# A graph kernel's row gathers issued without a write behind each, without waits for those writes, and at most two pairs ahead of TensorE

## The chip, the cores and the metric

The kernel runs on one core of a Trainium2 chip. The metric is the device time of one execution in microseconds. Of the kernel before there are three timed runs, and one further execution that the hardware profiler recorded.

## What is computed

A node has 128 features, there are 12500 nodes and 212500 edges `src -> dst`, sorted by `dst`, each of one of eight relation types. The kernel computes two relational layers, a layer norm, a graph layer with degree scaling and a second layer norm. Cut to what matters:

```python
def _rgcn_layer(x, W, SW, b, src, dst, rel):
    xt = jnp.einsum('nd,rde->rne', x, W)
    agg = jax.ops.segment_sum(xt[rel, src], dst, num_segments=x.shape[0])
    return jax.nn.relu(agg + x @ SW + b)
# L0: x1 = rgcn(x, w1, ...); x2 = rgcn(x1, w2, ...)       (sums 1 and 2)
x = _layernorm(x + L0(x))
# L1: feat = relu(x @ W1 + b1); h = feat * deg ** -0.5
#     agg = segment_sum(h[src], dst)                      (sum 3)
#     y = (feat - agg * deg ** -0.5) @ W2 + b2
x = _layernorm(x + L1(x))
```

So there are three sums over all edges, one after the other, and each needs, for every edge, the row of 128 floats of its source node: rows of `x` in sum 1, of `x1_d` in sum 2, of `h_d` in sum 3.

## The kernel before

**Gathers.** The edges are cut into 1661 tiles of 128. One gather, an indirect DMA issued by GpSimd (POOL), brings the 128 source rows of one tile from DRAM into one slot of `rows`, which has 56 slots. Seven tiles (`KG`) are a group, two groups (`PAIR`) a pair of 14 tiles, four pairs (`PR`) one pass of 56 tiles, which is once round the ring of slots. A sum has 29 full passes (`IT`) and a last one (`LEFT`) of 14, 14 and 9 tiles. 14 gathers of sum 2 and 21 of sum 3 are issued at the end of the sum before by `early` (L772); the other 4948 come from `run` (L802).

**What orders POOL's work.** `Gathers.run` is POOL's whole program in a sum, in order. Ahead of a pair it waits for `idx_ready` (ScalarE has copied the 14 columns of indices) and for `summed` (TensorE has used up the pair that decides). Which pair that is, `lead` says: with `lead=PR` it is the same pair of the pass before, so that POOL can be four pairs ahead of TensorE; with `lead=NEAR`, which is 2, it is the pair two before. The kernel before has `lead=PR` in passes 0 to 26, `NEAR + 1` in pass 27 and `NEAR` in pass 28 and in `LEFT`. Behind every gather stands a write of zeros to `pause`, which nobody reads (L806). The last write of a group (sums 1 and 2) or of a pair (sum 3) increments `paused`, and POOL waits for it ahead of the next one (`self.rest`).

**TensorE.** It waits for a whole group of landed rows, multiplies each tile with its one-hot matrix `r_S` (L990 in sums 1 and 2, L1214 in sum 3; an fp32 product is two MATMUL records, so a pair is x28), and signals `summed`. In sums 1 and 2 it runs in every pass, between pairs 0 and 1, the eight products with the relation weights (`mix`, L965), and around the pairs the steps of a tail that finishes 436 nodes. VectorE builds `r_S` for a pair when the pair two before is summed (L1051, L1244), adds the results into `acc`, and does the tail's elementwise work.

**Joins between sums.** `early` waits for the tail's stores (`stored`) and for `summed`; the next sum's other work waits for `over`, that is for all stores of the sum.

Of the kernel before, what the change touches and what calls it, by code (L numbers as in the profile page):

```python
# [12 lines left out]
P = 128  # L13
# [6 lines left out]
KG = 7  # L20
# [3 lines left out]
RING = 8  # L24
# [95 lines left out]
def build(nc, x, src, dst, rel, w1, sl1, b1, w2, sl2, b2, gw1, gb1, gw2, gb2, out):  # L120
    with ExitStack() as top:
        def sb(name, shape, dt=F32):
            return top.enter_context(nc.sbuf_tensor(name, shape, dt))


        def scratch(name, *shape):
            return nc.dram_tensor(name, shape, F32, kind="Internal").ap()

        x1_d, part_d, h_d = (scratch(n, N, D) for n in ("x1_d", "part_d", "h_d"))
        dinv_d = scratch("dinv_d", NPAD)  # L130


        c = Shared()
        c.W = [sb("w1s", [P, NREL, D]), sb("w2s", [P, NREL, D])]
        c.SL = [sb("sl1s", [P, D]), sb("sl2s", [P, D])]
        c.B = [sb("b1s", [P, 1]), sb("b2s", [P, 1])]
        c.GW = [sb("gw1s", [P, D]), sb("gw2s", [P, D])]
        c.GB = [sb("gb1s", [P, 1]), sb("gb2s", [P, D])]
        c.ident = sb("ident", [P, P])
        c.zeros_bf = sb("zeros_bf", [P, P], BF16)  # L140
        c.one_bf = sb("one_bf", [P, 1], BF16)
        c.eps = sb("eps", [P, 1])
        c.src_i = sb("src_i", [P, NT + UN], I32)
        c.rows = sb("rows", [P, UN, D])
        c.idx = sb("idx", [P, SETS * UN], I32)
        c.node = sb("node", [P, NT])
        c.relf = sb("relf", [P, NT])
        c.lo_b = sb("lo_b", [P, NT])
        c.glo = sb("glo", [P, NG])
        c.key = sb("key", [P, NT])  # L150
        c.gs = sb("gs", [P, NG])
        c.off_i = sb("off_i", [1, NGP, OFFS], I32)
        c.gs_i = sb("gs_i", [1, RING + NG], I32)
        c.gs8 = sb("gs8", [1, NG])
        c.step_t, c.step_g, c.carry = sb("step_t", [P, 1]), sb("step_g", [P, 1]), sb("carry", [P, 1])
        c.pause = sb("pause", [P, PT, P])
        c.found = sb("found", [SPOTS, DEG_COLS + COLS])
        c.deg = sb("deg", [DEG_ROWS, DEG_PARTS, NODES])
        c.dinv = sb("dinv", [P, NB])
        c.acc = sb("acc", [P, ACC])  # L160
        c.rounds_i = sb("rounds_i", [1, 2], I32)
        c.top = top
        c.passed = top.enter_context(nc.semaphore("passed"))
        c.over = top.enter_context(nc.semaphore("over"))
        c.psum = [top.enter_context(nc.psum_tensor(f"bank{i}", [P, BANK], F32)) for i in range(8)]
        c.iota = c.psum[IOTA_BANK][:, 0:TK]

        loads = [(c.W[0], w1.rearrange("r i o -> i r o")), (c.W[1], w2.rearrange("r i o -> i r o")),
                 (c.SL[0], sl1), (c.SL[1], sl2), (c.GW[0], gw1), (c.GW[1], gw2),
                 (c.B[0], b1.rearrange("(p a) -> p a", a=1)), (c.B[1], b2.rearrange("(p a) -> p a", a=1)),  # L170
                 (c.GB[0], gb1.rearrange("(p a) -> p a", a=1)), (c.GB[1], gb2.partition_broadcast(P))]
        c.early = early = Early(nc, top, c)
        last = Gathers(nc, top, c, "r3", h_d, 1, 2, 1, None)
        second = Gathers(nc, top, c, "r2", x1_d, 0, 1, PAIR, last)
        first = Gathers(nc, top, c, "r1", x, 0, 0, PAIR, second)
        with ExitStack() as ctx:
            prologue = Prologue(nc, ctx, c, early, Blocks(nc, ctx), (dst, src, rel), loads)
            tail = Tail1(nc, ctx, c, x, x1_d)
            one = relational_sum(nc, ctx, c, "r1", first, c.W[0], tail, prologue, None)
        with ExitStack() as ctx:  # L180
            tail = Tail2(nc, ctx, c, x, x1_d, part_d, h_d, dinv_d)
            two = relational_sum(nc, ctx, c, "r2", second, c.W[1], tail, None, early)
        with ExitStack() as ctx:
            tail = Tail3(nc, ctx, c, part_d, out)
            three = plain_sum(nc, ctx, c, last, tail, early)
        block = top.enter_context(nc.Block())

        @block.sync
        def _(sync):
            one.sync(sync)  # L190
            two.sync(sync)
            three.sync(sync)

        @block.scalar
        def _(act):
            one.scalar(act)
            two.scalar(act)
            three.scalar(act)

        @block.gpsimd  # L200
        def _(pool):
            one.gpsimd(pool)
            two.gpsimd(pool)
            three.gpsimd(pool)

        @block.tensor
        def _(pe):
            one.tensor(pe)
            two.tensor(pe)
            three.tensor(pe)  # L210

        @block.vector
        def _(dve):
            one.vector(dve)
            two.vector(dve)
            three.vector(dve)
# [484 lines left out]
class Gathers:  # L701
# [3 lines left out]
    def __init__(self, nc, top, c, tag, table, which, turns, incs, then):  # L705
        def sem(name):
            return top.enter_context(nc.semaphore(f"{tag}_{name}"))

        self.c, self.table, self.which, self.incs = c, table, which, incs
        self.most = N // GN + 2 if which else 4 * (N // GN + 1) + 1  # L710
        self.turns, self.then = turns, then
        self.rest = PAIR if then is None else 1
        self.landed = [sem(f"landed{h}") for h in range(RING + PAIR)]
        assert [s.num - self.landed[0].num for s in self.landed] == list(range(RING + PAIR))
        self.cleared = sem("cleared")
        self.paused = sem("paused")
        self.idx_ready = sem("idx_ready")
        self.summed = sem("summed")

# [56 lines left out]

    def run(self, pool, ready, stored):

        rest = self.rest

        def iteration(q, i, part, set_of, skip=0, lead=PR):
            at = set_of * UN
            for p in part.pairs:
                if (p + 1) * PT <= skip:
                    pool.sem_inc(self.paused, PAIR // rest)
                    continue
                pool.wait_ge(self.idx_ready, (q * (IT + 1) + i) * PR + p + 1)
                pool.wait_ge(self.summed, self.pairs_summed(q, i, p + PR - lead))  # L788
                gate(pool, self.c.passed)
                for h in range(p * PAIR, (p + 1) * PAIR):  # L790
                    if (h + 1) * KG <= skip:
                        if h % rest == rest - 1:
                            pool.sem_inc(self.paused, 1)
                        continue
                    if h % rest == 0:
                        pool.wait_ge(self.paused, q * (NG // rest) + i * (RING // rest) + h // rest + 1)  # L796
                        gate(pool, self.c.passed)
                    for k in range(part.of(h)):
                        s, slot = h * KG + k, h if k < halves(part, h) else RING + h % PAIR
                        if s < skip:  # L800
                            continue
                        pool.indirect_dma_start(  # L802
                            out=self.c.rows[:, self.place(s), :], out_offset=None, in_=self.table[:, :],
                            in_offset=bass.IndirectOffsetOnAxis(ap=self.c.idx[:, at + s:at + s + 1], axis=0)
                        ).then_inc(self.landed[slot], 16)
                        ins = pool.memset(self.c.pause[:, s % PT, :], 0.0)  # L806
                    if h % rest == rest - 1:
                        ins.then_inc(self.paused, 1)

        def one_round(q, skip=0):  # L810
            iteration(q, 0, FULL, 0, skip)
            with pool.Fori(0, IT // SETS - 1) as n:  # L812
                i = pool.snap(n * SETS)
                iteration(q, i + 1, FULL, 1)
                iteration(q, i + 2, FULL, 0)
            iteration(q, IT - 2, FULL, 1, lead=NEAR + 1)
            iteration(q, IT - 1, FULL, 0, lead=NEAR)
            iteration(q, IT, LEFT, 1, lead=NEAR)

        self.begin(pool)  # L820
        pool.sem_inc(self.cleared, 1)
        pool.sem_inc(self.paused, 1)
        one_round(0, EARLY[self.turns])
        if ready is not None:
            pool.wait_ge(ready, 1)
# [10 lines left out]
                pool.sem_inc(self.cleared, 1)  # L836
                one_round(q)
        pool.end_ifs()
        pool.wait_ge(self.paused, rounds * (NG // rest) + 1)
        gate(pool, self.c.passed)  # L840
        if self.then is not None:
            self.early(pool, rounds, stored)

# [976 lines left out]
```

## Time and profile before

| | |
|---|---|
| median of 3 runs | 7126.02 us (7123.88 to 7126.11) |
| profiled execution, its own time | 7141.85 us |
| its span | 7140.1 us |
| POOL busy | 5849.0 us (82%) |
| TensorE busy (matmul records) | 3398.9 us (48%) |
| VectorE / ScalarE busy | 1707.3 / 692.0 us |
| DMA share, mean of 16 engines, in each sum | 0.20, 0.20, 0.19 |

Engines are PE (TensorE), PEld (its weight loads), DVE (VectorE), ACT (ScalarE), POOL (GpSimd) and SP (SyncE). A row of a timeline gives the start, the duration, the engine, the line, the operation, and in brackets how long the engine had been idle before it and what ended that. A letter q behind an engine's name is its instruction queue. A POOL record of a gather covers the work of making it, not the landing of its data.

### The profile page before, as it was taken

To read this page: it belongs to the slowest core of one execution; us is meant where nothing else is said; L and a number is where in the kernel's file an instruction comes from. 1 tells how busy PE (TensorE), PEld (TensorE's weight loads), DVE (VectorE), ACT (ScalarE), POOL (GpSimd) and SP (SyncE) were. 2 spreads that over 40 slices of the span, in tenths; PEclk is the share of its full clock that TensorE was granted. 3 is DMA by queue.
4 is the path that set the end of the run, shared out by engine and by line. 5 is a ranking of instruction groups with operands and counts; after the bars stand their busy time and mean duration, and the time that the engine had idled before them with its cause. 6 is when DMAs were issued, how large, how long until landed. Compare 5 with 4: busy or idle time off the path is not lost.

```text
span 7140.1 us, 55913 instructions
## 1 busy us (share of the span) xinstructions
PE 3398.9 (48%) x12908; PEld 2515.0 (35%) x12909; DVE 1707.3 (24%) x2844; ACT 692.0 (10%) x1395; POOL 5849.0 (82%) x9940
## 2 busy tenths in 40 slices
PE   4455445554445655555554555554333333333333
PEld 3333333333333433333333333344333333333333
DVE  5333333333333312222222222221111111111111
ACT  2111111111111211111111111110000000000000
POOL 8888888888888788888888888878888888888887
PEclk7667666776667767777777777775555555555555
DMA  2111111111111212212222122221111111111111
GB/s 67 52 51 51 50 51 52 50 50 51 51 52 52 53 51 57 57 55 56 58 56 56 55 57 57 56 59 51 53 53 52 52 54 52 52 53 54 52 52 53
DMA packets 197671, 382.92 MB, mean 54 GB/s; under 512 B 84402, under 2 KB 93406, under 8 KB 197622
## 3 DMA queue, kind: packets, MB, share of 16 engines
q0 software_dynamic: 159456, 326.88, 17.5%
q1 hardware_dynamic: 36496, 54.67, 2.2%
q10 hardware_dynamic: 1670, 0.85, 0.0%
q8 instruction: 14, 0.23, 0.0%
q14 instruction: 35, 0.29, 0.0%
HBM read 356.43 MB, written 25.65 MB: 54 GB/s over the span
## 4 chain that ended last, share of the span: by engine, by line
POOL 78%; issue 20%; PE 1%; POOLq 1%; DMA 0%; DVE 0%; ACT 0%; DVEq 0%; SPq 0%; ACTq 0%
POOL rows L802 63%; POOL pause L806 15%; PE bank L965 0%; PE bank L990 0%; POOLq L112 0%; POOL rows L772 0%; PE bank L299 0%; DMA rows<-x_d,idx 0%; POOLq L788 0%; PE bank L1214 0%; PE bank L286 0%; POOLq L796 0%; DMA rows<-in_x_dram,idx 0%; POOLq L812 0%; DMA rows<-h_d,idx 0%
## 5 line engine op out<-in xcount | busy, mean ns | idle before, releaser
L990 PE MATMUL bank<-r_S,rows 128*128 128x128 f32 x6644 | 1361.7, 388 | 2125.9 <-DMA rows<-in_x_dram,idx 1065.1
L990 PEld LDWEIGHTS bank<-r_S,rows 128*128 128x128 f32 x6644 | 1259.3, 292 | 2271.9 <-issue 2271.6
L802 POOL DMA_INDIRECT rows<-in_x_dram,idx x1661 | 1587.6, 956 | 449.9 <-issue 258.2
L802 POOL DMA_INDIRECT rows<-x_d,idx x1647 | 1573.4, 955 | 444.0 <-issue 253.9
L802 POOL DMA_INDIRECT rows<-h_d,idx x1640 | 1565.0, 954 | 366.9 <-issue 272.0
L1214 PE MATMUL bank<-r_S,rows 128*128 128x64 f32 x3322 | 767.8, 424 | 1468.3 <-DMA rows<-h_d,idx 1462.0
L1214 PEld LDWEIGHTS bank<-r_S,rows 128*128 128x128 f32 x3322 | 726.2, 330 | 1513.7 <-DMA rows<-h_d,idx 925.2
L806 POOL MEMSET pause<- 128x128 f32 x4948 | 1097.1, 222 | 4.0
L1051 DVE TENSOR_TENSOR r_S<-bank,key 128x1792 f32<-128x1792 f32 x238 | 480.4, 2019 | 1219.8 <-PE bank L990 1219.2
L917 ACT COPY r_agg<-bank 128x512 f32<-128x512 f32 x476 | 278.2, 584 | 3961.9 <-PE bank L965 2066.5
L1271 DVE TENSOR_TENSOR acc<-acc,bank 128x64 f32 x238 | 52.9, 222 | 1920.2 <-PE bank L1214 1904.4
L965 PE MATMUL bank<-r_agg,w1s 128*128 128x512 f32 (+1 forms) x528 | 458.5, 1037 | 4.5 <-ACT bank L580 4.5
L965 PE MATMUL bank<-r_agg,w2s 128*128 128x512 f32 (+1 forms) x528 | 457.8, 1035 | 4.7 <-ACT bank L580 4.7
L1046 DVE TENSOR_TENSOR r_hot<-bank,b_spot 128x1344 bf16<-128x1344 f32 x119 | 185.4, 1558 | 1145.0 <-PE bank L990 1142.7
L1090 DVE TENSOR_TENSOR acc<-acc,bank 128x64 f32 x492 | 109.2, 222 | 802.3 <-PE bank L965 745.6
L1049 DVE TENSOR_REDUCE r_placed<-r_hot 128x192 bf16<-128x1344 bf16 x119 | 288.3, 2422 | 4.1
L580 ACT CAST bank<-zeros_bf 128x512 f32<-128x512 bf16 x480 | 282.1, 588 | 21.4 <-DVEq L571 6.4
L965 PEld LDWEIGHTS bank<-r_agg,w1s 128*128 128x128 f32 x528 | 115.2, 224 | 319.5 <-issue 319.3
L965 PEld LDWEIGHTS bank<-r_agg,w2s 128*128 128x128 f32 x528 | 113.1, 218 | 317.8 <-issue 317.3
L746 ACT COPY idx<-src_i x360 | 71.2, 202 | 1015.7 <-PE bank L1214 964.6
L1244 DVE TENSOR_TENSOR r_S<-bank,key 128x896 f32<-128x896 f32 x119 | 129.8, 1092 | 36.4 <-DVE acc L1271 36.3
L1746 ACT ACTIVATE d_sd<-d_mv,eps 109x4 f32<-109x4 f32 (+2 forms) x29 | 8.6, 297 | 1277.0 <-DVEq L1766 1277.0
(151 smaller groups left out, 1384.4 us busy)
## 6 DMA issues: line engine op xcount, KB each, us to landing
rows<-in_x_dram,idx POOLq DMA_INDIRECT x1661, 2.6
rows<-x_d,idx POOLq DMA_INDIRECT x1647, 3.5
rows<-h_d,idx POOLq DMA_INDIRECT x1640, 2.5
d_xr<-in_x_dram SPq DMA_DIRECT2D x54, 218.0 KB
x_d<-d_yr SPq DMA_DIRECT2D x27, 218.0 KB
d_x1r<-x_d SPq DMA_DIRECT2D x27, 218.0 KB
h_d<-d_hr SPq DMA_DIRECT2D x27, 218.0 KB
part_d<-d_pr SPq DMA_DIRECT2D x27, 218.0 KB
```

The lines of the kernel that those rows point to most:

```text
L580: return act.copy(ap, c.zeros_bf[0:ap.shape[0], 0:1].broadcast_to([*ap.shape]))
L802: pool.indirect_dma_start(out=self.c.rows[:, self.place(s), :], out_offset=None, in_=self.table[:, :], in_offset=bass.IndirectOffsetOnAxis ...
L806: ins = pool.memset(self.c.pause[:, s % PT, :], 0.0)
L917: act.copy(agg[:, h, :, :], agg_ps[h % BUFS][:, :].rearrange("p (n r) -> p n r", r=NREL)).then_inc(taken, 1)
L965: mm = pe.matmul(mix_ps[:, 0:groups * GN], W[:, r, :], agg[:, first:first + groups, :, r], start=(r == 0), stop=(r == NREL - 1))
L990: mm = pe.matmul(agg_ps[j][:, bass.ds(offs[j * KG + k], TK)], c.rows[:, g.place(h * KG + k), :], S[:, pb, j * KG + k, :], start=False, sto ...
L1046: ch.then(dve.tensor_tensor(hot[:, b, :, :], spots.unsqueeze(1).broadcast_to([P, PT, SPOTS]), bc_last(blocks.spot[:, at], SPOTS), ALU.is_e ...
L1049: dve.tensor_reduce(placed[:, b, :, :], hot[:, b, :, :].rearrange("p (j k) n -> p j n k", k=KG), AX.X, ALU.add)
L1051: dve.tensor_tensor(S[:, b, :, :], c.iota[:, :].unsqueeze(1).broadcast_to([P, PT, TK]), bc_last(c.key[:, at], TK), ALU.is_equal).then_inc( ...
L1090: ins = dve.tensor_tensor(window, window, mix_ps[:, w * GN:(w + 1) * GN], ALU.add)
L1214: mm = pe.matmul(sum_ps[b][:, j * GN:(j + 1) * GN], c.rows[:, g.place(h * KG + k), :], S[:, b, j * KG + k, :], start=(k == 0), stop=(k == ...
L1244: dve.tensor_tensor(S[:, p % BUFS, :, :], c.iota[:, 0:GN].unsqueeze(1).broadcast_to([P, PT, GN]), bc_last(c.key[:, bass.ds(i * UN + p * PT ...
```

## The change

The writes to `pause`, the buffer, the semaphore `paused`, its increments and all waits for it go away. The passes 1 to 28, an even number, are all in one loop and all have `lead=NEAR`; pass 0 keeps `lead=PR` and `LEFT` keeps `NEAR`. The gathers themselves, their tables, indices, slots and semaphores stay.

```diff
-        c.pause = sb("pause", [P, PT, P])
...
-        self.rest = PAIR if then is None else 1
...
                 pool.wait_ge(self.idx_ready, (q * (IT + 1) + i) * PR + p + 1)
                 pool.wait_ge(self.summed, self.pairs_summed(q, i, p + PR - lead))
                 gate(pool, self.c.passed)
                 for h in range(p * PAIR, (p + 1) * PAIR):
-                    if (h + 1) * KG <= skip:
-                        if h % rest == rest - 1:
-                            pool.sem_inc(self.paused, 1)
-                        continue
-                    if h % rest == 0:
-                        pool.wait_ge(self.paused, q * (NG // rest) + i * (RING // rest) + h // rest + 1)
-                        gate(pool, self.c.passed)
                     for k in range(part.of(h)):
...
                         ).then_inc(self.landed[slot], 16)
-                        ins = pool.memset(self.c.pause[:, s % PT, :], 0.0)
-                    if h % rest == rest - 1:
-                        ins.then_inc(self.paused, 1)
...
             iteration(q, 0, FULL, 0, skip)
-            with pool.Fori(0, IT // SETS - 1) as n:
+            with pool.Fori(0, IT // SETS) as n:
                 i = pool.snap(n * SETS)
-                iteration(q, i + 1, FULL, 1)
-                iteration(q, i + 2, FULL, 0)
-            iteration(q, IT - 2, FULL, 1, lead=NEAR + 1)
-            iteration(q, IT - 1, FULL, 0, lead=NEAR)
+                iteration(q, i + 1, FULL, 1, lead=NEAR)
+                iteration(q, i + 2, FULL, 0, lead=NEAR)
             iteration(q, IT, LEFT, 1, lead=NEAR)
...
-        pool.wait_ge(self.paused, rounds * (NG // rest) + 1)
-        gate(pool, self.c.passed)
```

On POOL, where pass 0 of sum 1 ends and the loop over the passes begins, the rows before are these (`rows` is the ring of slots, `r1_` marks a semaphore of sum 1):

```order
L802 DMA rows<-in_x_dram,idx 128x128
L806 MEMSET pause 128x128
L812 UNCONDITIONAL_BRANCH
L812 ISA
L788 ISA [waits r1_idx_ready]
L796 REGISTER_ALU [waits r1_summed]
L802 DMA rows<-in_x_dram,idx 128x128 [waits r1_paused]
L806 MEMSET pause 128x128
```

In the changed kernel, where L789 is the gather and the loop is L796, the same place reads:

```order
L789 DMA rows<-in_x_dram,idx 128x128 x13
L796 UNCONDITIONAL_BRANCH
L796 ISA
L782 ISA [waits r1_idx_ready]
L789 DMA rows<-in_x_dram,idx 128x128 [waits r1_summed]
L789 DMA rows<-in_x_dram,idx 128x128 x13
```

Gathers now follow each other directly, and a pair's first gather has the waits for `idx_ready` and `summed` alone; the value that `summed` must reach there is two pairs higher. The order of the instructions on TensorE, VectorE, ScalarE and SyncE is the same in both kernels but for the line numbers.

## Rows read from the trace of the kernel before

**Rows 1.** The page: busy time by engine, and the chain that ended last

```profile
PE 3398.9 (48%) x12908; PEld 2515.0 (35%) x12909; DVE 1707.3 (24%) x2844; ACT 692.0 (10%) x1395; POOL 5849.0 (82%) x9940
...
POOL 78%; issue 20%; PE 1%; POOLq 1%; DMA 0%; DVE 0%; ACT 0%; DVEq 0%; SPq 0%; ACTq 0%
```

**Rows 2.** Groups of POOL instructions: line, operation, count | busy us, mean ns

```profile
L802 POOL DMA_INDIRECT rows<-in_x_dram,idx x1661 | 1587.6, 956 | 449.9 <-issue 258.2 <-POOL pause L806 191.6
...
L806 POOL MEMSET pause<- 128x128 f32 x4948 | 1097.1, 222 | 4.0
```

**Rows 3.** Waits of POOL, whole span: us in total, times, longest us

```profile
POOL rows L802 <- issue: 784.2, 4358, 2.6
POOL rows L802 <- POOL pause L806: 476.5, 589, 0.9
```

**Rows 4.** Timeline of POOL in the middle of sum 1

```profile
1028.54 0.95 POOL L802 DMA_INDIRECT rows<-in_x_dram,idx  x1 [0.81 <-POOL pause L806]
...
1029.87 0.95 POOL L802 DMA_INDIRECT rows<-in_x_dram,idx  x1 [0.16 <-issue]
...
1036.57 0.95 POOL L802 DMA_INDIRECT rows<-in_x_dram,idx  x1 [0.17 <-issue]
```

**Rows 5.** The gathers of L772, and their timeline ahead of sum 2

```profile
L772 POOL DMA_INDIRECT rows<-h_d,e_idx x21: 943/947/952, 4808.3 to 4833.3; - x21
...
2407.80 0.95 POOL L772 DMA_INDIRECT rows<-x_d,e_idx  x1 [2.43 <-issue]
...
2424.07 0.95 POOL L772 DMA_INDIRECT rows<-x_d,e_idx  x1 [0.30 <-issue]
2425.32 0.94 POOL L802 DMA_INDIRECT rows<-x_d,idx  x1 [0.30 <-issue]
```

**Rows 6.** Timeline of POOL: first and last gather after a gap of 1.07

```profile
171.56 0.96 POOL L802 DMA_INDIRECT rows<-in_x_dram,idx  x1 [1.07 <-issue]
...
7118.72 0.95 POOL L802 DMA_INDIRECT rows<-h_d,idx  x1 [1.07 <-issue]
```

**Rows 7.** Timeline of POOL: first gathers of pass 0 and pass 1, sum 1

```profile
4.53 1.10 POOL L802 DMA_INDIRECT rows<-in_x_dram,idx  x1 [2.63 <-issue]
...
89.21 0.95 POOL L802 DMA_INDIRECT rows<-in_x_dram,idx  x1 [0.82 <-POOL pause L806]
```

**Rows 8.** Timeline of PE in pass 0 of sum 1

```profile
69.89 4.97 PE L990 MATMUL bank<-r_S,rows 128*128 128x128 f32 x28
74.70 14.86 PE L965 MATMUL bank<-r_agg,w1s 128*128 128x512 f32 x16
...
97.34 3.37 PE L990 MATMUL bank<-r_S,rows 128*128 128x128 f32 x28
```

**Rows 9.** Timeline of PE at the start of sum 2, pairs 0 to 2

```profile
2444.80 5.33 PE L990 MATMUL bank<-r_S,rows 128*128 128x128 f32 x28 [9.52 <-issue]
...
2466.47 8.16 PE L990 MATMUL bank<-r_S,rows 128*128 128x128 f32 x56 [1.65 <-ACT bank L580]
```

**Rows 10.** Timeline of POOL, first gather of a pair 1 in sum 2

```profile
3071.35 0.95 POOL L802 DMA_INDIRECT rows<-x_d,idx  x1 [0.81 <-POOL pause L806]
```

**Rows 11.** Timeline of PE in the same pass, end of pair 0 to pair 1

```profile
3075.17 3.35 PE L990 MATMUL bank<-r_S,rows 128*128 128x128 f32 x14 [7.19 <-DMA rows<-x_d,idx]
...
3079.76 14.87 PE L965 MATMUL bank<-r_agg,w2s 128*128 128x512 f32 x16
3096.29 5.01 PE L990 MATMUL bank<-r_S,rows 128*128 128x128 f32 x28 [1.66 <-ACT bank L580]
```

**Rows 12.** A long gather at the start of sum 3

```profile
4847.22 1.73 POOL L802 DMA_INDIRECT rows<-h_d,idx  x1 [0.17 <-issue]
```

**Rows 13.** The VectorE instruction beside it

```profile
4846.22 1.90 DVE L1253 TENSOR_TENSOR key<-node,gs 128x1666 f32<-128x1666 f32 x1
```

**Rows 14.** The page: DMA queue of the gathers, packets, MB, share of 16 engines

```profile
q0 software_dynamic: 159456, 326.88, 17.5%
```

More of the change, by code:

```diff
@@ L715, in __init__ @@
         self.cleared = sem("cleared")
-        self.paused = sem("paused")
         self.idx_ready = sem("idx_ready")
@@ L777, in run @@
     def run(self, pool, ready, stored):
-        rest = self.rest
         def iteration(q, i, part, set_of, skip=0, lead=PR):
@@ L784, in iteration @@
                 if (p + 1) * PT <= skip:
-                    pool.sem_inc(self.paused, PAIR // rest)
                     continue
@@ L821, in run @@
         pool.sem_inc(self.cleared, 1)
-        pool.sem_inc(self.paused, 1)
         one_round(0, EARLY[self.turns])
```

## The prediction

> **What bounds the kernel now.** I read the page first. POOL is busy 5849.0 us of 7140.1, and the chain that ended last is POOL for 78% and "issue" for 20%, while TensorE has 1% of it [rows 1]. So the time is the time in which POOL gets its 4983 gathers out, one after the other. The groups of POOL instructions say what it does: a gather is 956 ns of busy time, and each of the 4948 of L802 is followed by a write of 222 ns [rows 2]. The waits say what lies between: short "issue" gaps, and 589 waits for a write to `pause`, 476.5 us in all or 0.81 us each [rows 3]. No wait of POOL for TensorE of any size is in that list. The timeline gives the rhythm: a group's gathers start 1.338 us apart ((1036.57 - 1028.54) / 6), made of 0.95 for the gather, 0.22 for the write and 0.17 of gap [rows 4].
>
> **The writes.** Taking away 222 ns does not gain 222 ns. The trace holds 35 gathers that have no write behind them, those of L772. They too last 0.947 us, and the gap between two of them is not 0.17 but 0.30: 14 starts from 2407.80 to 2424.07 are 1.2515 us apart [rows 5]. The gain is thus 1.338 - 1.252 = 0.086 us for a gather, and for 4948 of them 426 us. The bounds: if the whole write went, 1097 us [rows 2]; if the gap grew to fill its place, nothing. I take 426, because the same instruction stands in rows 5 in the same order as in the changed kernel.
>
> **The waits for the writes.** A waiting gather has a gap of 0.81 where its neighbours have 0.17 [rows 4]. That is 0.64 us more, and for 589 waits [rows 3] 377 us. Every second one of sums 1 and 2, and every one of sum 3, stands at a pair's head, where the waits for `idx_ready` and `summed` stay. They were met long before, and such waits seem to cost nothing: the first gather of L802 in sum 2 is behind three of them and still has a gap of 0.30 [rows 5]. The bounds are 0 and 0.64 us for some 357 pair heads, 228 us; I take 0. [...]
>
> Together that is 803 us gross. The 1.07 us gaps, one in every 70 gathers, 69 in all [rows 6], have no write or wait in them that goes away; I keep all. If they went too, that would be another 69 x (1.07 - 0.17) = 62 us.
>
> **The shorter lead, at a sum's start.** Here is the one loss that I expect. In sum 1 POOL begins at 4.53 and reaches the first gather of pass 1 at 89.21 [rows 7]. With the gains above (56 x 0.086 and eight waits of 0.64, 9.9 us) it would come there at 79.3. Before, that gather needed pair 0 to be summed, done at 74.9; now it needs pair 2. TensorE does not owe that to the gathers: it has pair 0, then 14.86 us of L965, then pair 1, and ends pair 2 at 97.34 + 3.37 = 100.7 [rows 8]. POOL stands still for 21.4 us, and since it is the bound, all of that is lost. In sum 2 pairs 1 and 2 end at 2466.47 + 8.16 = 2474.6 [rows 9], 66.8 us after the first early gather at 2407.80 [rows 5]; POOL arrives 56 x 1.252 = 70.1 us after it. TensorE's own end of sum 1 may take 2 us of the difference, so it is nearly free. In sum 3 there is no product with weights between the pairs, so I expect none either. I charge 2 us for both, with 0 and 10 as bounds.
>
> **The shorter lead, in every pass.** Behind POOL's wait for `summed` stand all further gathers, and TensorE waits for those. The pair that is summed latest after its rows are there is pair 1, since L965 stands ahead of it. In the pass of sum 2 shown, pair 1's first gather starts at 3071.35 [rows 10] and TensorE is through with it at 3096.29 + 5.01 = 3101.3, 30.0 us later [rows 11]. In the changed kernel, pair 3's first gather is wanted 28 x 1.252 = 35.1 us after that start. Since pair 0's end is then about half a microsecond later against it, 4.6 us of slack stay. L965 already runs at 14.87 us here [rows 11], the same as in pass 0 [rows 8], so I do not expect it to get slower. This costs 0; without the slack each microsecond would cost 28 us in a sum.
>
> **Gathers that get longer.** One gather took 1.73 us [rows 12] while VectorE ran an operation with two SBUF inputs from 4846.22 to 4848.12 [rows 13]. Such cases are few: what the 1661 gathers of sum 1 have above 0.95 each is 1587.6 - 1578 = 10 us [rows 2], so some 30 us in the three sums, and they are in both kernels. Denser gathers meet the same operations of VectorE more often by 7126 / 6350, 12%, which is 3 us; I charge 0 and leave it to the range.
> [...]
>
> **The sum.** 426 + 377 - 21.4 - 2 = 780 us. The profiled execution took 7141.85 us, so it would take 6362. Its time is 15.8 us above the median of the runs, 7126.02, and I take the same off: 6346, which I give as 6347, 10.9% less.
>
> **Rivals.**
> - *The pair heads stay visible* (0.07). The wait for `summed` holds the queue even when met, because its value is computed in registers in the loop. For it: in the trace all loop heads lie under a wait for `pause`, so no row shows one bare. Against: the gap of 0.30 in rows 5. At the full 0.64 us it gives back 228 us: 6575.
> - *The lead binds in every pass* (0.08). The 4.6 us of slack are used up, because rows land later when gathers are denser. At 3 us over in each of 28 passes of sum 2, it gives back 84 us: 6431. Against: the queue of the gathers fills only 17.5% of the DMA engines [rows 14].
> - *The write was hidden* (0.03). The gap grows from 0.17 to 0.39 in a long run, so that the change does not do what it says for the writes; only the waits are gained: about 6347 + 426 = 6773.
> - *The 1.07 us gaps go too* (0.04): 6285.
> [...]
>
> **Chances.** 0.70 for the forecast, with a range of its own of 6310 to 6400: at the low end about half of the 1.07 us gaps are gone, at the high end 50 us of stalls are added. The range for 8 in 10 takes in the lead that binds in every pass and somewhat more than half of the pair heads' price, and reaches down to the case without the 1.07 us gaps: 6285 to 6480. It leaves out the slower case, the full pair heads and the hidden write. A measurement of this kernel tells about 0.2%, 14 us, from no change. All cases but the slow one are faster, 0.90 with a little off for what I have not thought of; the same 0.02; slower 0.08.
>
> **What would show it.** POOL's gathers, L789 then, at starts 1.25 us apart with gaps of 0.30, also at the heads of pairs. No row of POOL waiting for `pause`. One wait of POOL for TensorE of about 21 us near 79 to 101 us, and next to none later; many short ones in sum 2 would show the lead binding. The chain that ended last still POOL and issue for over 95%, now gathers alone. The forecast is wrong if the gathers' own mean rises above 0.96, if their distance is not 1.25 in long runs, or if POOL has waits for TensorE beyond 30 us in all.

## The result, and the profile after

The changed kernel takes 6278.23 us (median of 4 runs, 6273.37 to 6279.88), the kernel before 7125.6 us beside it (4 runs, 7123.88 to 7126.11). The ratio is 0.881, with a 95% interval of 0.8795 to 0.8825: 847 us or 11.9% less. Forecast were 6347 us and a range of 6285 to 6480, so the change gained 69 us more than I forecast, and the time lies 7 us below the range.

The page of the changed kernel answers to [rows 1, 2, 14]; its profiled execution took 6273.37 us:

```profile
span 6271.6 us, 50257 instructions
PE 3351.0 (53%) x12908; PEld 2481.7 (40%) x12909; DVE 1704.4 (27%) x2844; ACT 691.4 (11%) x1395; POOL 4716.1 (75%) x4992
...
q0 software_dynamic: 159456, 326.88, 19.9%
...
POOL 57%; issue 21%; PE 13%; DMA 7%; DVE 1%; ACT 0%; POOLq 0%; SPq 0%; DVEq 0%; ACTq 0%; PEldq 0%
...
L789 POOL DMA_INDIRECT rows<-in_x_dram,idx x1661 | 1573.1, 947 | 526.5 <-issue 484.5
```

POOL has lost its 4948 writes and nothing else; the same packets and bytes leave it in 12% less time. A gather's record lasts 0.947 us in the mean of sum 1, and its rows land 2.6 us after its start (median):

```profile
rows<-in_x_dram,idx POOLq DMA_INDIRECT x1661, 2.6
```

POOL's waits, beside [rows 3]:

```profile
POOL rows L789 <- issue: 1463.8, 4803, 0.7
POOL rows L789 <- PE bank L969: 51.0, 108, 18.4
POOL rows L789 <- PE bank L1193: 10.4, 34, 0.3
```

4803 short gaps make 1463.8 us, 0.305 each. TensorE is named as releaser 142 times, but 18.4 of those 61.4 us are one wait. The others have the gap that a gather has anyway. This one is the gather 116 of sum 1 (gathers are counted from 0), the fifth of its pair, where the program has no wait at all:

```profile
172.86 0.94 POOL L789 DMA_INDIRECT rows<-in_x_dram,idx  x1 [0.30 <-PE bank L969]
```

TensorE is named there because POOL's instruction queue works ahead of the gathers: its record of the wait of the next pair, ten gathers on, stands at 172.7, just ahead of this gather. How far ahead the queue is can be read where the loop turns. The queue's branch to the pass that begins with gather 168 stands at 222.6, and that gather starts at 237.76, with twelve others between (a row of the queue gives the shortest, the median and the longest duration in ns, then the first and the last start in us):

```profile
L796 POOLq COMPARE_BRANCH  x1: 53/53/53, 222.6 to 222.6; - x1
...
237.76 0.94 POOL L789 DMA_INDIRECT rows<-in_x_dram,idx  x1 [0.30 <-issue]
```

At the 42 such branches of the three sums it is ten to twelve gathers ahead.

So the chain, which now gives PE and DMA 20% of the span, would mislead by itself: it follows a gather back to its releaser even where the gap ahead of it is no longer than the usual 0.30. The prediction had wanted over 95% for POOL and issue there; by the gaps that holds, by the chain it does not.

The one true stop of any size is at the head of pass 1 of sum 1, the place that the prediction named:

```profile
78.58 0.94 POOL L789 DMA_INDIRECT rows<-in_x_dram,idx  x1 [0.30 <-issue]
97.94 0.94 POOL L789 DMA_INDIRECT rows<-in_x_dram,idx  x1 [18.43 <-PE bank L969]
99.19 0.94 POOL L789 DMA_INDIRECT rows<-in_x_dram,idx  x1 [0.30 <-issue]
```

What is missing is the point. Of 4982 gaps between gathers 4978 are 0.30 to 0.32 us. The four others are this stop, two gaps of 2.7 and 2.6 around the start of sum 3, and 0.67 at the head of pass 1 of sum 2; none is 1.07. The 69 long gaps [rows 6] are gone, though they had neither a write nor a wait in them. In the kernel before they stand ahead of a pair's second gather, at the gathers 113, 183, 253, ... of each sum, 70 apart; here gather 113 has 0.30 like its neighbours.

### The profile page after: what moved, and what is told of

Same layout as the page of the kernel before. It is cut to its first block, busy times and chain, and to the rows that moved or that the text cites. A ratio compares the mean times of both kernels' runs of the same rounds, so it can differ in the third digit from the quotient of the medians.

```text
span 6271.6 us, 50257 instructions
## 1 busy us (share of the span) xinstructions
PE 3351.0 (53%) x12908; PEld 2481.7 (40%) x12909; DVE 1704.4 (27%) x2844; ACT 691.4 (11%) x1395; POOL 4716.1 (75%) x4992
## 4 chain that ended last, share of the span: by engine, by line
POOL 57%; issue 21%; PE 13%; DMA 7%; DVE 1%; ACT 0%; POOLq 0%; SPq 0%; DVEq 0%; ACTq 0%; PEldq 0%
POOL rows L789 57%; PE bank L969 7%; PE bank L944 4%; DMA rows<-in_x_dram,idx 3%; DMA rows<-h_d,idx 2%; DMA rows<-x_d,idx 2%; PE bank L1193 1%; DMA acc<-in_dst_dram 0%; ACT r_agg L896 0%; PE bank L1435 0%; ACT bank L579 0%; POOLq L782 0%; SPq L386 0%; PE bank L1564 0%; POOLq L781 0%
## 5 line engine op out<-in xcount | busy, mean ns | idle before, releaser
L969 PE MATMUL bank<-r_S,rows 128*128 128x128 f32 x6644 | 1334.4, 383 | 1555.1 <-DMA rows<-in_x_dram,idx 778.7
L789 POOL DMA_INDIRECT rows<-in_x_dram,idx x1661 | 1573.1, 947 | 526.5 <-issue 484.5
L789 POOL DMA_INDIRECT rows<-x_d,idx x1647 | 1556.0, 945 | 502.2 <-issue 490.3
L789 POOL DMA_INDIRECT rows<-h_d,idx x1640 | 1552.8, 947 | 501.9 <-issue 489.0
L969 PEld LDWEIGHTS bank<-r_S,rows 128*128 128x128 f32 x6644 | 1239.3, 288 | 1684.6 <-issue 1684.5
L1193 PEld LDWEIGHTS bank<-r_S,rows 128*128 128x128 f32 x3322 | 726.1, 330 | 1264.6 <-DMA rows<-h_d,idx 801.4
L963 PEld LDWEIGHTS bank<-one_bf,r_placed 128*96 128x96 bf16 x238 | 32.7, 157 | 124.6 <-issue 120.5
```

The lines of the kernel that those rows point to most:

```text
L789: pool.indirect_dma_start(out=self.c.rows[:, self.place(s), :], out_offset=None, in_=self.table[:, :], in_offset=bass.IndirectOffsetOnAxis ...
L969: mm = pe.matmul(agg_ps[j][:, bass.ds(offs[j * KG + k], TK)], c.rows[:, g.place(h * KG + k), :], S[:, pb, j * KG + k, :], start=False, sto ...
L1193: mm = pe.matmul(sum_ps[b][:, j * GN:(j + 1) * GN], c.rows[:, g.place(h * KG + k), :], S[:, b, j * KG + k, :], start=(k == 0), stop=(k == ...
```

## The experiments

Two questions are open. How much of the 847 us is each part of the change? And what took the long gaps away: that the writes are gone, that the waits are gone, or the shorter lead? Where a diff of POOL's program stands below it is against the changed kernel, unless it says "of before". "Before" in brackets is the kernel before on the same chip.

### The writes without a stop

A 128x128 write behind every gather again, in a buffer of its own. The wait lags one group, so that POOL never stands at it.

```diff
+                    pool.wait_ge(self.paused, q * NG + i * RING + h + 1)
+                    gate(pool, self.c.passed)
...
                         ).then_inc(self.landed[slot], 16)
+                        ins = pool.memset(self.c.pause0[:, s % PT, :], 0.0)
+                    ins.then_inc(self.paused, 1)
...
+        pool.sem_inc(self.paused, 2)
```

> The changed kernel with the 128x128 write put back behind every gather, and no wait at which POOL stands: the wait for the writes is for those of the group before the last one, which ended some 9 us earlier. Lead as in the changed kernel. All theories: gathers 1.338 us apart instead of 1.2495, so 4948 x 0.0885 = 438 us more. Theory W (the 1.07 us gaps, one in 70 gathers, come with the writes, because POOL then has two instructions for each gather): the gaps are back, 69 x 0.9 = 62 us, in all 6278 + 500 = 6778. Rival P (they come with the waits for the writes, which stop the queue): no such gaps, 6716.

Measured: 6698.51 us (6695.67 to 6701.14; 4 runs), ratio to before 0.9402 (0.9386 to 0.9417). POOL's timeline in the middle of sum 1:

```profile
1000.79 0.95 POOL L797 DMA_INDIRECT rows<-in_x_dram,idx  x1 [0.17 <-issue]
1001.74 0.22 POOL L801 MEMSET pause<- 128x128 f32 x1
1002.12 0.95 POOL L797 DMA_INDIRECT rows<-in_x_dram,idx  x1 [0.17 <-issue]
```

The rhythm of [rows 4] is back, 1.33 us, and 4948 writes cost 6698.5 - 6278.2 = 420 us, 0.085 each (426 forecast). What is left up to the kernel before on the same chip, 7125.1 - 6698.5 = 427 us, is for the waits, the long gaps and the lead. There are no long gaps: the writes do not make them.

### The waits without most of the writes

The kernel before with the leads of the changed one; only the last write of each group or pair stays, and all waits for them.

```diff
 (of before)
-                        ins = pool.memset(self.c.pause[:, s % PT, :], 0.0)
+                        if h % rest == rest - 1 and k == part.of(h) - 1:
+                            ins = pool.memset(self.c.pause[:, s % PT, :], 0.0)
```

> The kernel before, with the lead of the changed one and only the last write of a group left; all its waits for that write stay (one a group in sums 1 and 2, one a pair in sum 3). Each wait costs 0.95 + 0.22 + 0.81 - 1.25 = 0.73 us, 595 of them 434 us. Theory W: the 1.07 us gaps are gone or rarer than one in 100 gathers, 6712. Rival P: they stand every 70 gathers, 6774.

Measured: 6764.15 us (6762.9 to 6766.36; 4 runs), ratio 0.9493 (0.9477 to 0.9509). POOL's waits and its timeline at the 113th gather:

```profile
POOL rows L802 <- POOL pause L807: 475.3, 588, 0.9
```

```profile
176.85 0.95 POOL L802 DMA_INDIRECT rows<-in_x_dram,idx  x1 [0.81 <-POOL pause L807]
179.06 0.95 POOL L802 DMA_INDIRECT rows<-in_x_dram,idx  x1 [1.27 <-issue]
180.32 0.94 POOL L802 DMA_INDIRECT rows<-in_x_dram,idx  x1 [0.30 <-issue]
```

The long gaps are back, 69 of them, every 70 gathers. It is the waits that show them. The bill: a write and a wait take 0.22 + 0.81 where 0.30 was, 588 x 0.73 = 429 us, and 69 x 0.97 = 67 us for the long gaps, together 496 us; measured 6764.2 - 6278.2 = 486.

### A shorter write, and a second one

As the first experiment, with a write of 128x1 (`pause0` is `[P, PT, 1]`):

> As the kernel 'writes', but the write behind each gather is of 128x1 instead of 128x128. If the length of the write adds to that of the gather and the gap of 0.17 stays, gathers are 0.95 + 0.10 + 0.17 = 1.22 us apart, which is 0.03 less than without a write: 6278 - 148 = 6130, and 6192 with the 1.07 us gaps (theory W). Rival: the preparation of the next gather takes 0.30 after a gather whatever stands between, so that a short write is hidden: 1.25 apart, 6278, or 6340 with the gaps.

Measured: 6272.26 us (6268.92 to 6273.76), ratio 0.8803 (0.8788 to 0.8817). On the timeline:

```profile
1000.92 0.94 POOL L797 DMA_INDIRECT rows<-in_x_dram,idx  x1 [0.19 <-issue]
1001.86 0.11 POOL L801 MEMSET pause<- 128x1 f32 x1
1002.17 0.94 POOL L797 DMA_INDIRECT rows<-in_x_dram,idx  x1 [0.19 <-issue]
```

4948 short writes cost nothing: the gather starts 0.30 after the end of the one ahead, with or without them.

As the first experiment, with a 128x1 write behind the 128x128 one, one run:

```diff
+                        ins = pool.memset(self.c.pause0[:, s % PT, :], 0.0)
+                        ins = pool.memset(self.c.pause1[:, s % PT, :], 0.0)
```

> As the kernel 'writes', with a second write, of 128x1, behind the first: three POOL instructions a gather. Only the profile matters. Theory W, if it is the number of instructions that counts (140 between two gaps in the kernel before): a gap of about 1.07 us every 47 gathers, 105 in all. If it counts gathers with any write: every 70, as before. Rival P: none. Time by W near 6778 + 33 + 4948 x 0.1 to 0.13, 7300 to 7450.

Measured: 6864.61 us, not the 7300 to 7450 expected. A 128x1 write costs another 166 us over the first experiment or 0.034 each, since it starts before the long one is over:

```profile
1000.27 0.23 POOL L802 MEMSET pause<- 128x128 f32 x1
1000.41 0.12 POOL L803 MEMSET pause<- 128x1 f32 x1
1000.70 0.95 POOL L798 DMA_INDIRECT rows<-in_x_dram,idx  x1 [0.16 <-issue]
```

So writes do not add up by their durations. This kernel too has no long gap every 70 gathers, with two writes behind each.

### The lead alone

The changed kernel with the leads of before (before: 7141.17 on this chip, 15 runs):

```diff
-            with pool.Fori(0, IT // SETS) as n:
+            with pool.Fori(0, IT // SETS - 1) as n:
...
-                iteration(q, i + 1, FULL, 1, lead=NEAR)
-                iteration(q, i + 2, FULL, 0, lead=NEAR)
+                iteration(q, i + 1, FULL, 1)
+                iteration(q, i + 2, FULL, 0)
+            iteration(q, IT - 2, FULL, 1, lead=NEAR + 1)
+            iteration(q, IT - 1, FULL, 0, lead=NEAR)
```

> The changed kernel with the lead of the kernel before (four pairs in passes 0 to 26, then three, then two), still without writes and waits for them. The one stop of POOL for TensorE, 18.4 us ahead of pass 1 of sum 1, goes away, and nothing else changes: 6278 - 18 = 6260. Rival (the shorter lead does something for the gathers that go without a write, such as keeping them short): the mean of a gather rises above 0.947 us and the time is 6278 or more.

Measured: 6266.48 us (6257.37 to 6269.55; 5 runs), ratio 0.8776 (0.8764 to 0.8788). It ran again beside the changed kernel itself, on one chip (before: 7126.36, 9 runs):

> The changed kernel itself, on the same chip and beside the same runs of the kernel before as the next one, since the kernel before took 7141 us on one chip and 7125 on another. Ratio to before 0.881.

> The changed kernel with the lead of the kernel before, beside the changed kernel. If the shorter lead costs the 18.4 us for which POOL stands at the start of sum 1, this is 18 us faster than the changed kernel (0.3%), ratio to before 0.8785; if the lead costs nothing, the two are equal.

Measured: the changed kernel 6275.76 us (6275.32 to 6281.85; 5 runs), ratio 0.8807 (0.8795 to 0.8819); with the old leads 6256.59 us (6255.71 to 6257.29; 5 runs), ratio 0.8779 (0.8767 to 0.8791). The difference is 19.2 us, and no run of the one reaches the other. All that the shorter lead does is the stop at the head of pass 1, with next to nothing at that place in sum 2. POOL's waits for TensorE with the old leads:

```profile
POOL rows L789 <- PE bank L971: 0.3, 1, 0.3
```

This version beats both kernels.

The other way round, the kernel before with the new leads (the same diff with its signs changed), on the chip of the first of these runs:

> The kernel before with the lead of the changed one alone; all writes and waits stay. POOL comes to pass 1 of sum 1 at 89.2 and pair 2 is summed at 100.7, so it stands for 11.5 us there and nowhere else: 7125 + 11.5 = 7137, with the 1.07 us gaps as before. Rival (the lead takes the 1.07 us gaps away): 7137 - 62 = 7075.

Measured: 7154.1 us (7149.71 to 7156.51; 11 runs), ratio 1.0017 (1.0008 to 1.0026), so 12.9 us slower. POOL's waits:

```profile
POOL rows L802 <- POOL pause L806: 475.6, 587, 0.9
POOL rows L802 <- PE bank L988: 11.9, 1, 11.9
```

The stop is there and shorter, since POOL comes later to it. The long gaps are all there too: the lead does not remove them.

### Is it the write, or the stop?

If the waits show the long gaps because POOL's queue stands still there, a stop for TensorE must show them as well, without any write. The changed kernel with `lead=1` in the loop and in `LEFT`, one run:

```diff
-                iteration(q, i + 1, FULL, 1, lead=NEAR)
-                iteration(q, i + 2, FULL, 0, lead=NEAR)
-            iteration(q, IT, LEFT, 1, lead=NEAR)
+                iteration(q, i + 1, FULL, 1, lead=1)
+                iteration(q, i + 2, FULL, 0, lead=1)
+            iteration(q, IT, LEFT, 1, lead=1)
```

> The changed kernel with a lead of one pair in passes 1 to 28 and in LEFT: POOL really stands for TensorE at each pair's head, some 5 us in sums 1 and 3 and 8 in sum 2, so about 348 heads x 6 = 2100 us more, 8400. What it is for are the gaps: if any stop of POOL's queue makes them visible, there is one of about 1.26 us in every 70 gathers, behind a pair's head; if it takes a wait for POOL's own write, there is none.

Measured: 8440.25 us. POOL's waits, and its timeline at one of the places:

```profile
POOL rows L789 <- PE bank L969: 1463.7, 224, 29.5
POOL rows L789 <- PE bank L1193: 711.2, 112, 8.7
```

```profile
199.71 0.94 POOL L789 DMA_INDIRECT rows<-in_x_dram,idx  x1 [5.76 <-PE bank L969]
201.93 0.95 POOL L789 DMA_INDIRECT rows<-in_x_dram,idx  x1 [1.27 <-issue]
203.18 0.94 POOL L789 DMA_INDIRECT rows<-in_x_dram,idx  x1 [0.30 <-issue]
```

No write and no `pause` in the program, and the gap of 1.27 stands again at the gathers 113, 183, ..., one gather behind a stop. Both kinds of stop that the runs have just ahead of the place, for a write and for TensorE, show it, with 0.97 us above the usual 0.30.

Does any stop do, or only one just ahead of the place? The changed kernel with one write behind the third gather of each group and a wait for it ahead of the fourth, one run:

```diff
+                        if k == 2 and part.of(h) > 3:
+                            pool.memset(self.c.pause[:, :], 0.0).then_inc(self.paused, 1)
+                            pool.wait_ge(self.paused, q * NG + i * RING + h + 1)
+                            gate(pool, self.c.passed)
```

> The changed kernel with one 128x128 write behind the third gather of every group and a wait for it ahead of the fourth, nothing at the heads. Each wait costs 0.73 us as in 'waits', some 710 of them 520 us: 6278 + 520 + 62 = 6860 with the long gaps. If the long gap belongs to whatever gather follows a stop at the right moment, it moves behind the fourth gather of a group; if it belongs to a pair's head, it stays at the second gather of a pair or vanishes (6798).

Measured: 6795.52 us, 6798 expected without the gaps. POOL stands 706 times, more often than in the kernel before:

```profile
POOL rows L794 <- POOL pause L799: 570.0, 706, 1.0
```

```profile
189.65 0.22 POOL L799 MEMSET pause<- 128x128 f32 x1
190.68 0.95 POOL L794 DMA_INDIRECT rows<-in_x_dram,idx  x1 [0.81 <-POOL pause L799]
191.93 0.95 POOL L794 DMA_INDIRECT rows<-in_x_dram,idx  x1 [0.30 <-issue]
```

No long gap is left: it did not move to the gather behind a stop, which was one of the two ways expected. The second gather of a pair, where it stood, lies five gathers behind such a stop. This run by itself leaves open that the gap belongs to a stop at a pair's head.

In between: one write behind the 13th gather of each pair, and the wait ahead of the 14th, so that the second gather of the next pair lies two behind it. One run (before: 7126.36):

```diff
+                        if h % PAIR == PAIR - 1 and k == part.of(h) - 2:
+                            pool.memset(self.c.pause[:, :], 0.0).then_inc(self.paused, 1)
+                            pool.wait_ge(self.paused, q * NGP + i * PR + p + 1)
+                            gate(pool, self.c.passed)
```

> The changed kernel with one 128x128 write behind the 13th gather of every pair and a wait for it ahead of the 14th: POOL's queue stops two gathers before the place where the long gaps were (the second gather of a pair). 357 waits of 0.73 us, 260 us: 6538. If being ahead by two gathers is enough to hide what happens there, no gap of 1.2 us or more; if not, some 69 of them, and 62 us more, 6600.

Measured: 6570.91 us, between the two sums expected. At 60 of the 69 places the gap is 0.60 to 0.87, mostly 0.72, neither the 0.30 of a hidden one nor 1.27; at the other nine it is 1.07 to 1.11. What the 69 have above 0.30 makes 32 us, which is what the time has above 6538. One of the nine:

```profile
539.14 0.95 POOL L792 DMA_INDIRECT rows<-in_x_dram,idx  x1 [0.81 <-POOL pause L797]
540.39 0.94 POOL L792 DMA_INDIRECT rows<-in_x_dram,idx  x1 [0.30 <-issue]
542.45 0.94 POOL L792 DMA_INDIRECT rows<-in_x_dram,idx  x1 [1.11 <-issue]
```

So a stop that is not at a pair's head shows the gap too, at the same place. The extra time falls with the distance from the last stop: 0.97 us one gather behind it, mostly 0.4 two behind, none five behind.

The queue's own records show what is hidden. In the kernel of the waits, the queue's next record behind the stop at a pair's head is the one of L796 for the next group, seven gathers on. Here is a pair without a long gap, and then the one with the long gap at gather 183:

```profile
196.75 0.95 POOL L802 DMA_INDIRECT rows<-in_x_dram,idx  x1 [0.81 <-POOL pause L807]
L796 POOLq ALU_OP  x1: 32/32/32, 199.4 to 199.4; - x1
...
272.52 0.95 POOL L802 DMA_INDIRECT rows<-in_x_dram,idx  x1 [0.81 <-POOL pause L807]
L796 POOLq ALU_OP  x1: 32/32/32, 276.9 to 276.9; - x1
```

The queue gets through the seven gathers in 2.65 us, while the gathers themselves take 1.25 us each; that is how it comes to be ahead. With the place among them it takes 4.40 us. These are also the medians of 87 and 24 such stretches; with `lead=1`, where the next record is 14 gathers on, they are 5.93 and 7.68 us. So the queue stands 1.75 us longer at the place in both kernels, and the gap of 1.27 shows 0.97 of it.

### What comes every 70 gathers

The kernel of the waits with one more gather per pair from pass 1 on, into a buffer that nobody reads, and with the passes 1 and 2 written out ahead of the loop. If the place is a count of gathers, it moves against the pairs; if it goes by pairs, it stays every fifth one. One run:

```diff
+                pool.indirect_dma_start(
+                    out=self.c.spare[:, p % 2, :], out_offset=None, in_=self.table[:, :],
+                    in_offset=bass.IndirectOffsetOnAxis(ap=self.c.src_i[:, 0:1], axis=0)
+                ).then_inc(self.spared[p % 2], 16)
...
-            with pool.Fori(0, IT // SETS) as n:
+            iteration(q, 1, FULL, 1, lead=NEAR)
+            iteration(q, 2, FULL, 0, lead=NEAR)
+            with pool.Fori(1, IT // SETS) as n:
```

> The kernel 'waits' with one gather more in every pair of passes 1 to 29, ahead of its last one, into a buffer that nobody reads (345 in all; its rows are not used), so that a pair has 15 gathers. Time 6764 + 345 x 1.25 = 7195. If the long gap comes with every 70th gather, the visible ones at a pair's head are no longer 5 pairs apart (70 is not a multiple of 15), and there are about a third as many; if it comes with every fifth pair, they are 75 gathers apart and as many as before.

Measured: 7255.44 us, 7195 expected. The long gaps are now 2.3 us and come every 60 gathers, which is every four pairs of 15:

```profile
263.81 0.95 POOL L816 DMA_INDIRECT rows<-in_x_dram,idx  x1 [2.31 <-issue]
```

Both readings fell. There are 81 of them, all at the first gather of a pass, from pass 3 on, where the loop begins; the other pairs' heads have 0.81. This kernel changes several things at once (the extra wait, a second destination, the loop), so it says no more than that. In the others the distance is 70 gathers with 70 writes between (the kernel before), with five to ten (the waits) or with none (`lead=1`), so it is not a count of all of POOL's instructions; and the loop has 112 gathers, so it is not one place in the program either. What the queue does there stays open.

## Why the prediction was right in its mechanism and missed in one term

**The writes: right.** 426 us forecast, 420 measured by the first experiment. To take the gap between two gathers of `early` from [rows 5] was the step that carried it; the write's own 0.22 would have given 1097.

**The waits: right.** 377 us for 589 waits. The waits for `idx_ready` and `summed` at the pairs' heads cost nothing, as taken: 0.30 in the rows above, also at the heads in the loop, where the value for `summed` is computed in registers. That rival, 228 us dearer, fell, and so did that of the hidden write. No run takes the waits alone away. The nearest is the first experiment, which has all the writes and the new lead: the kernel before is 427 us above it, and 377 for the waits and 62 for the long gaps, less 17 for that run's stop at pass 1, make 422.

**The long gaps: wrong, and the step that failed.** "The 1.07 us gaps, one in every 70 gathers, 69 in all [rows 6], have no write or wait in them that goes away; I keep all." The premise is true and the conclusion is not. Once in 70 gathers POOL's queue took 1.75 us longer in the kernel of the waits (4.40 against 2.65) and with `lead=1` (7.68 against 5.93). One gather behind a stop 0.97 us of it show; five gathers behind one, and in the changed kernel with its queue ten to twelve gathers ahead, nothing does. My reading is that the time is over there before the gathers that the queue has already handed on are made. Whether it is the gathers or the time since the stop that counts, no run separates. In the kernel before, the wait for `pause` at each pair's head stood one gather ahead of every such place. So 69 of those waits each cost 0.64 us at its own row and another 0.90 one row later (1.07 against the 0.17 of a gather behind a write), 62 us that I had worked out and given 0.04 as a rival. The gap had been seen one row behind a wait each time it came; that was the sign to read.

**The stop at the head of pass 1: right in place, cause and size.** 21.4 us forecast; 18.43 - 0.30 = 18.1 in the profiled execution above. POOL came when expected, at 79.5. TensorE was early: it ended pair 2 at 97.1, not at 100.7. TensorE's timeline beside [rows 8]:

```profile
90.30 3.39 PE L969 MATMUL bank<-r_S,rows 128*128 128x128 f32 x28
...
93.74 3.39 PE L969 MATMUL bank<-r_S,rows 128*128 128x128 f32 x28
```

Pair 1's product had taken 6.16 us in the kernel before. The difference shows in the views of both kernels in stretches (length, busy us and instructions of PE, PEld, DVE, ACT, POOL, then TensorE's granted clock, DMA share, GB/s). First before, then after:

```profile
91.00:97.00 6.00, 5.88 (x29) 5.91 (x30) 1.41 (x7) 2.16 (x4) 5.34 (x10) 0.50 0.19 49
```

```profile
90.00:93.60 3.60, 3.42 (x30) 3.34 (x30) 1.41 (x7) 2.22 (x4) 0.00 (x0) 1.00 0.01 2
```

The granted clock was 0.50 there and is 1.00 here. Pair 1's product is 2.8 us shorter with it, of the 3.6 us, and the rest is an earlier start of pair 0. But that is no effect of the change. The changed kernel was profiled a second time, beside the old leads, and there the clock fell as in the kernel before:

```profile
92.00:98.00 6.00, 6.00 (x30) 5.99 (x31) 1.11 (x6) 1.76 (x3) 0.00 (x0) 0.51 0.00 1
```

```profile
91.84 6.27 PE L969 MATMUL bank<-r_S,rows 128*128 128x128 f32 x28
```

```profile
102.21 0.94 POOL L789 DMA_INDIRECT rows<-in_x_dram,idx  x1 [21.58 <-PE bank L969]
```

The stop is 21.3 us in this execution, the forecast. TensorE had done the same in all three before it, the product with the relation weights for 14.86 us and a pause of about 1.5; why the clock fell in two and not in the third is not shown. At the head of pass 1 of sum 2, where I had called the lead nearly free, POOL loses 0.4 us in the first execution and 1.2 in the second.

**Every other pass: right.** The slack of pair 1 in sum 2 was forecast at 4.6 us. TensorE and POOL in such a pass, beside [rows 10, 11], first TensorE:

```profile
2687.59 14.85 PE L944 MATMUL bank<-r_agg,w2s 128*128 128x512 f32 x16
2704.09 4.85 PE L969 MATMUL bank<-r_S,rows 128*128 128x128 f32 x28 [1.66 <-ACT bank L579]
```

```profile
2679.18 0.94 POOL L789 DMA_INDIRECT rows<-x_d,idx  x1 [0.30 <-issue]
...
2714.13 0.94 POOL L789 DMA_INDIRECT rows<-x_d,idx  x1 [0.30 <-issue]
```

Pair 1's first gather is at 2679.18, TensorE is through with the pair at 2708.9, and pair 3's first gather, which needs that, starts at 2714.13: 5.2 us of slack. The lead binds nowhere but at the two heads of pass 1: at every other pair of both executions the queue is through its wait for TensorE 3.1 us or more before the pair's first gather starts, and at the stops it is 0.8. I had charged 23.4 us for it in all; the run with the old leads says 19.2.

**Longer gathers: none.** They got shorter, a mean of 947 ns against 956 in sum 1 [rows 2], and they follow at 1.2485 us, not 1.252. The slower case fell with that: for it, gathers without a break between them would have had to follow at more than 1.252 + 780 / 4948 = 1.41 us.

**The sum.** 420 for the writes, 377 for the waits, 62 for the long gaps, less 19 for the lead: 840 of the 847 us measured. With my own terms it had been 780. My range ended at 6285, which is my own sum with the long gaps gone and nothing to spare, so that errors of a few us in the other terms were enough to fall below it.

## What to carry to other kernels

A gap that looks bare of any cause may be the shadow of a stop a few instructions ahead of it: before you keep it in a sum, look whether it always stands at the same distance behind a wait, and price both cases in the range. A wait in a queue that otherwise runs ahead can cost more than its own row shows: here 69 of the 589 waits cost 0.64 us at their own row and 0.90 at the next. A releaser named beside a gap of the usual length, here 0.30, is no stop. And two parts of a change are worth running apart: here the shorter lead cost 19 us for nothing, and the old leads with the writes and waits gone are the fastest version, 6256.6 us.

## What the runs showed of the hardware

- POOL's next gather starts 0.30 us after the end of the one ahead if nothing or a 0.11 us write stands between; a 0.22 us write moves it by 0.085 only, and a second short write by another 0.034.
- To wait for a write of POOL's own costs 0.64 us (a gap of 0.81 against 0.17), a wait for another engine that the queue has passed 3.1 us or more before the gather behind it starts nothing that can be seen.
- POOL's queue is ten to twelve gathers ahead at the loop's branches of the changed kernel; behind a stop in the kernel of the waits it gets through seven gathers in 2.65 us.
- Once in 70 gathers it takes 1.75 us more there and with `lead=1`. Of this 0.97 us show one gather behind a stop, mostly 0.4 two behind, and none five behind.
- Gathers of 128 rows hold 1.2485 us from start to start for 1000 in a row in sum 1 of the changed kernel, with no stretching.
- TensorE's product of pair 1 took 6.16 us at a granted clock of 0.50 and 3.39 us at 1.00, and two executions of the same kernel differ in this: 3.39 and 6.27 us.
